# Hybrid S6/MoE/S5/MoE block: the expert layers moved by two slots, one sum and one normalisation moved to VectorE

## The chip, the cores and the metric

One NeuronCore of one Trainium2 chip runs the whole program. The metric is device time in microseconds, lower is better. Five engines take part: TensorE (PE; its weight loads are PEld), VectorE (DVE), ScalarE (ACT), GpSimd (POOL) and SyncE (SP), which issues nearly all DMAs.

## What is computed

The input x has 8 batches of 512 tokens with 128 channels, float32. Four residual layers follow each other, each on a layer-normed input:

```python
x = x + attn_a(layernorm(x))   # S6: silu(x Wi) -> d, B, C; delta = softplus(d Wdt)
                               # h_t = exp(delta_t A) h_{t-1} + delta_t B_t x_t, 256 channels x 64 states
                               # y = C * sum(h) + xs*Dp; y * silu(res) @ Wo; + residual; layernorm * gamma + beta
x = x + ffn(layernorm(x))      # 8 experts, the 2 largest logits, their softmax as weights
                               # sum_e weight_e * (silu(x W1_e) * (x W2_e)) @ W3_e
x = x + attn_b(layernorm(x))   # S5: 64 complex states, a diagonal scan, plus D*u
x = x + ffn(layernorm(x))      # the same experts again
```

All eight experts are computed for all tokens; `rt[:, 0]` holds each token's weight of each expert (zero for six of them).

## The kernel before, in words

**Turns and slots.** The S6 scan is the long part: 256 channels x 64 states x 512 steps are 128 scans ("pairs") of a 128x512 tile for each batch. The program runs 8 *turns*, one batch's 128 pairs each, and each pair is a *slot*. For pair k, ACT writes the decay `da = exp(dr * A)` into PSUM (L837), POOL the product `w = ur * br` of two pairs at once, a duo (L947), and DVE scans `h = da*h + w` (L1251). PE sums four scanned pairs into `ys` (`sum_states`, L633). The rings between them are short: `da` holds 4 pairs, `w` 5 duos, `h` 6 duos.

**What rides on the slots.** Every other piece of work is a generator that yields the slot at which it wants to be issued. `weave` (L210) puts them in each engine's own instruction stream: first the pair of the slot, then the tasks due, in the order gates, late, post, pre. Engines run their stream strictly in order and meet only through semaphores. A task whose slot is 128 or more is issued at the end of the turn, ahead of the next turn's first pair (the last loop of `weave`). In turn b the "pre" tasks prepare batch b+1 (layer norm, projections, delta, C), the "post" tasks do batch b-1 from `z` (the output projection) through the first MoE, S5 and the first part of the second MoE, and the "late" tasks finish the second MoE of batch b-2. After turn 7 two turns with no scan follow (the tail).

**The MoEs.** `MOE_AT` gives the slot where MoE 1 and MoE 2 begin (28 and 105). Each has four quarters of four tiles, 11 slots apart: `h` tiles (W1) and `g` tiles (W2) on PE (L565), silu on ACT (L785), the product `aq` on DVE (L1189). Expert e's output `y` is 8 pairs of matmuls on PE (L579); ACT scales it by the weights into `yk` (L798), POOL adds it to the residual tile (`expert_sums`, L890). `y`, `z` and the transposes share PSUM bank Y; the `h`/`g` tiles use banks H, G and sometimes Y. For MoE 2, tiles 8 to 15 and experts 3 to 7 are late: tiles 8 to 11 fall on slot 0 of the next turn, experts 3 to 7 on slots 0, 7, 14, 18, 23. Expert 2 of MoE 2 has slot 125 on PE and slot 131 in POOL's sum, so that sum stands at the end of the turn, before the next turn's first product.

**Last sum.** The 32nd sum of a turn (of pairs 124 to 127) is issued on PE by `tail()` (L641) at slot 128, thus ahead of the next turn's opening tiles. DVE's `take_sums(c, 1)` (L1127, slot 1 of the next turn) multiplies `ys` by the gate; PE's `z` (L583, slot 5) uses it; DVE adds the residual at slot 7 and takes the moments of layer norm 1 (L1093).

**Layer norms.** DVE takes moments, POOL computes rstd and -mean*rstd (`rstd`, L849), ACT applies them (`normalize`, L694) with four 128x128 activations. For layer norm 1 POOL then multiplies by gamma (L899) and adds the residual (L902).

**Routing.** DVE finds the two largest logits by a chain of 14 small operations (L1136). Intermediate tiles `R(1)`, `R(3)`, `R(5)` lie in SBUF, the others in the PSUM bank. The weights are built from a tanh of the half gap, as twice their value, and W3 is halved once: POOL does that in turn 0 (`scale_outputs`, L860, four operations of 128x512).

**Start.** Before turn 0 the projections of batch 0 run. DVE computes `delta` (L1120) behind the S5 matrix setup (L1029 to L1066, slot PRE_AT+10), and POOL's `du = delta * xs` (L878) waits until all four input tiles, the two of the residual branch (`sres`) included, are drained. SP stores delta and du to HBM (L357, L363) and loads them back spread over partitions (L368); the first product needs that load.

## Time and profile before

| | us |
|---|---|
| time, median of 3 runs (lowest, highest) | 1849.11 (1846.08, 1857.18) |
| profiled execution, its own time | 1861.63 |
| its span | 1859.7 |
| mean granted TensorE clock | 0.86 of full |
| first scan starts | 55.1 |
| turns 0 to 7, from first scan to last | 1641 |
| tail after the last scan | 164 |
| DVE, POOL, PE, ACT busy | 1514.5, 1513.9, 1351.0, 1281.5 |

The page has the engines' busy times, the span in 40 slices, the chain that ended last, and the costliest groups of instructions by line. The chain is spread thin: PE 27%, ACT 18%, DVE 15%, POOL 14%. "Idle" in a row is the time its engine stood still just before the instruction, with what released it. Consecutive DVE instructions overlap by about 0.08 us in the records, so a scan of 1.2 us advances the clock by 1.13.

### The profile page before, as it was taken

The numbers are of one execution on the slowest core, as the hardware profiler recorded it, in microseconds if no ns is written. First come the engines' busy times: TensorE is split into PE (matmuls) and PEld (weight loads), VectorE is DVE, ScalarE is ACT, GpSimd is POOL, SyncE is SP. The second block draws the span as 40 slices with busy tenths as digits, with TensorE's granted clock in tenths as the row PEclk, the third lists the DMA queues.
The fourth block names the chain that finished last, engine by engine and source line by source line (L and its number), as shares of the span: only waits on it lengthen the run. The fifth ranks groups of instructions, "written<-read, shape, count | busy, mean of one in ns | idle before, by whom it ended". The sixth has DMA issues, their size and how long they took to land.

```text
span 1859.7 us, 19053 instructions
## 1 busy us (share of the span) xinstructions
PE 1351.0 (73%) x5928; PEld 617.7 (33%) x5928; DVE 1514.5 (81%) x2105; ACT 1281.5 (69%) x2275; POOL 1513.9 (81%) x888
## 2 busy tenths in 40 slices
PE   4336458777886887778776878778787778668958
PEld 1001123234342343324342343324332343324535
DVE  4879988898889889898899888888888988895222
ACT  4547668687877778777777778777787777755423
POOL 0899999978998799977998899987998799983312
PEclk9557569889987989879897989879898898979979
DMA  3601411122111311132101401132111321100000
GB/s 87 212 34 71 164 46 51 49 91 97 57 40 48 148 51 33 54 104 96 55 25 50 162 29 51 49 106 81 51 51 49 102 85 52 46 29 1 7 1 6
DMA packets 38747, 121.89 MB, mean 66 GB/s; under 512 B 5875, under 2 KB 21110, under 8 KB 26358
## 3 DMA queue, kind: packets, MB, share of 16 engines
q1 hardware_dynamic: 37062, 120.67, 18.3%
q8 instruction: 47, 0.77, 0.2%
q14 instruction: 54, 0.44, 0.1%
q10 hardware_dynamic: 1584, 0.01, 0.0%
HBM read 109.13 MB, written 11.53 MB: 65 GB/s over the span
## 4 chain that ended last, share of the span: by engine, by line
PE 27%; ACT 18%; DVE 15%; POOL 14%; issue 8%; DVEq 0%; POOLq 0%; ACTq 0%
DVE h L1251 10%; POOL w L947 9%; PE bankH L565 8%; ACT da L837 5%; PE bankY L579 5%; PE bankG L565 5%; ACT yk L798 4%; ACT L837 3%; PE ys L633 2%; POOL x L890 2%; PE bankG L512 2%; DVE aq L1189 1%; PE bankY L559 1%; ACT L785 1%; ACT sq L785 1%
## 5 line engine op out<-in xcount | busy, mean ns | idle before, releaser
L1251 DVE TENSOR_TENSOR_SCAN h<-da,w 128x512 f32<-128x512 f32 x1024 | 1192.1, 1206 | 158.3 <-ACT da L837 133.0
L947 POOL TENSOR_TENSOR w<-ur,br 128x1024 f32<-128x1024 f32 x512 | 1193.6, 2365 | 33.1 <-DVE h L1251 21.2
L837 ACT ACTIVATE da<-dr,al 128x511 f32<-128x511 f32 x1024 | 681.9, 687 | 221.9 <-DVE h L1251 212.5
L633 PE MATMUL ys<-h,wsum 128*32 128x512 f32 x2048 | 320.9, 703 | 208.5 <-DVE h L1251 189.2
L565 PE MATMUL bankH<-nT,w 128*128 128x512 f32 x512 | 301.8, 673 | 89.7 <-DVE aq L1189 85.3
L890 POOL TENSOR_TENSOR x<-x,yk 128x512 f32<-128x512 f32 x128 | 163.1, 1274 | 211.2 <-ACT yk L798 210.6
L579 PEld LDWEIGHTS bankY<-w,aq 128*128 128x128 f32 x2048 | 262.8, 203 | 87.0 <-issue 65.0
L579 PE MATMUL bankY<-w,aq 128*128 128x128 f32 x2048 | 270.5, 289 | 12.4 <-DVE aq L1189 7.9
L565 PE MATMUL bankG<-nT,w 128*128 128x512 f32 x432 | 243.8, 648 | 24.6 <-DVE aq L1189 24.6
L798 ACT ACTIVATE yk<-bankY,rt 128x128 f32<-128x128 f32 x512 | 151.8, 364 | 121.5 <-PE bankY L579 107.8
L633 PEld LDWEIGHTS ys<-h,wsum 128*32 128x32 f32 x2048 | 42.9, 115 | 408.5 <-DVE h L1251 373.2
L565 PEld LDWEIGHTS bankH<-nT,w 128*128 128x128 f32 x512 | 87.0, 205 | 243.5 <-DVE aq L1189 147.9
L565 PEld LDWEIGHTS bankG<-nT,w 128*128 128x128 f32 x432 | 80.1, 203 | 163.9 <-issue 89.0
L512 PE MATMUL bankG<-xs,wx 128*128 128x512 f32 x64 | 44.3, 829 | 38.5 <-DVE sres L1115 37.7
L1189 DVE TENSOR_TENSOR aq<-tq,bankH 128x512 f32<-128x512 f32 x64 | 42.7, 667 | 35.3 <-PE bankH L565 35.3
L785 ACT ACT_TABLE_LOAD x55 | 70.6, 1283 | 1.0
L837 ACT ACT_TABLE_LOAD x54 | 69.3, 1283 | 1.0
L1189 DVE TENSOR_TENSOR aq<-tq,bankG 128x512 f32<-128x512 f32 x64 | 42.5, 665 | 32.2 <-PE bankG L565 32.1
L699 ACT ACTIVATE nrm<-x,nm,rs 128x128 f32<-128x128 f32 x96 | 39.4, 480 | 31.5 <-POOL nm L858 31.5
L852 POOL TENSOR_TENSOR var<-bag,eps 128x4 f32<-128x4 f32 x40 | 8.5, 212 | 59.0 <-DVE bag L1100 59.0
L785 ACT ACTIVATE tq<-bankH 128x512 f32<-128x512 f32 x64 | 38.3, 599 | 25.2 <-PE bankH L565 24.9
L785 ACT ACTIVATE sq<-bankH 128x512 f32<-128x512 f32 x64 | 38.2, 597 | 23.2 <-PE bankH L565 23.2
(187 smaller groups left out, 1135.8 us busy)
## 6 DMA issues: line engine op xcount, KB each, us to landing
br<-b_rows SPq DMA_DIRECT2D x64, 1024.0 KB, 5.0
dr<-d_rows SPq DMA_DIRECT2D x16, 1024.0 KB, 7.1
ur<-u_rows SPq DMA_DIRECT2D x16, 1024.0 KB, 8.4
d_rows<-vh SPq DMA_DIRECT2D x16, 256.0 KB
u_rows<-th SPq DMA_DIRECT2D x16, 256.0 KB
xnew<-in_L_attn_a_x_dram SPq DMA_DIRECT2D x8, 256.0 KB, 5.3
w<-in_L_ffn_W_dram SPq DMA_DIRECT2D x2, 1024.0 KB, 11.1
x<-in_L_attn_a_x_dram SPq DMA_DIRECT2D x8, 256.0 KB, 9.1
```

What stands on the lines that cost most here:

```text
L512: ins = nc.tensor.matmul(p[:, :], lhs(k), xs[:, k, :], start=(k == 0), stop=(k == 1))
L565: is_filled(t, f"{name}{m}_{n}", nc.tensor.matmul(p[:, :], wt[:, n // 2, n % 2 * 128:n % 2 * 128 + 128], nT[:, :], start=True, stop=True))
L579: ins = nc.tensor.matmul(p[:, a * 128:(a + 1) * 128], aq[:, (2 * n + k) % 4, a * 128:(a + 1) * 128], w3[:, n, k, :], start=(k == 0), stop= ...
L633: ins = nc.tensor.matmul(ys[32 * q:32 * q + 32, :], wsum[:, :], h[:, (DUOS * t.b + 2 * group + q // 2) % H_RING, q % 2, :], start=(n == 0) ...
L699: A(dst[:, a, :], src[:, a, :], ACT.Identity, bias=nm[:, k, a:a + 1], scale=rs[:, k, a:a + 1]).then_inc(normed[k], 1)
L785: A(zt[j % 4], p[:, :], ACT.Silu).then_inc(drained[BANK[f"h{m}_{j}"]], 1)
L798: ins = A(yk[:, a, :], p[:, a * 128:(a + 1) * 128], ACT.Copy, scale=rt[:, 0, a, e:e + 1])
L837: A(da[duo % D_RING][:, k % 2, 1:L], dr[:, half, q, 1:L], ACT.Exp, scale=nega[:, QUADS * half + q, n:n + 1]).then_inc(decay_ready, 1)
L890: G.tensor_tensor(total[:, :, :], total[:, :, :], yk[:, :, :], ALU.add).then_inc(added, 1)
L947: G.tensor_tensor(w[:, turn_duo % W_RING, :, :], ur[:, half, q:q + 2, :], br[:, chunk % B_RING, row:row + 1, :].to_broadcast([128, 2, L]), ...
L1189: drain(f"g{m}_{n}", V.tensor_tensor(aq[:, n % 4, :], zt[n % 4], p[:, :], ALU.mult))
L1251: V.tensor_tensor_scan(h[:, turn_duo % H_RING, k % 2, :], da[duo % D_RING][:, k % 2, :], w[:, turn_duo % W_RING, k % 2, :], 0.0, ALU.mult, ...
```

## The change

MoE 1 and 2 begin at slots 30 and 107, the pre tasks and layer norms 1 and 2 are two slots later too. Tiles 8 to 11 of the second MoE get slots 1, 1, 2, 2 (their `g` tiles 4, 5, 8, 9), late experts slots 5, 9, 16, 20, 25. The last sum of a turn moves on PE to slot 2 of the next turn. `take_sums` goes to slot 3, `z` to slot 6. A quarter's four silus are issued together. Layer norm 1 is applied by DVE with four `tensor_scalar`. The last expert of MoE 1 is weighted and added by DVE with four `scalar_tensor_tensor` on PSUM, so neither ACT nor POOL takes part. The weights have their own scale, W3 is not halved; for this the routing's `R(5)` (SBUF) is multiplied in SBUF by `rc`, which a new 128x4 `tensor_scalar` prepares. In the start, the S5 setup on DVE goes behind delta, and du of batch 0 waits for two input tiles only.

```diff
-MOE_AT = {1: 28, 2: 105}
+MOE_AT = {1: 30, 2: 107}
...
 FIRST_LATE_TILE, FIRST_LATE_OUTPUT = 8, 3
-LATE_OUTPUTS = {3: 0, 4: 7, 5: 14, 6: 18, 7: 23}
+LATE_OUTPUTS = {3: 5, 4: 9, 5: 16, 6: 20, 7: 25}
...
 THREE_STEPS = (2, 4, 7, 8)
+AT_TURN = ((1, 1, 2, 2), (4, 5, 8, 9))
+TAKE_AT = 3
...
-    at = silu_at(m, j) + step
-    return max(0, at - PAIRS) if is_late_tile(m, j) else at
+    at = silu_at(m, j)
+    if is_late_tile(m, j) and at < PAIRS + QUADS:
+        return AT_TURN[step > 0][j % 4]
+    return at - PAIRS + step if is_late_tile(m, j) else at + step
...
 GATES_AT, RES_AT = 44, 54
-PRE_AT = 70
+PRE_AT = 72
 SETUP_ROWS_AT = PRE_AT + 9
-SETUP_AT = PRE_AT + 10
-MATRICES_AT = PRE_AT + 11
+SETUP_AT = PRE_AT + 17
+MATRICES_AT = PRE_AT + 17
 TURN_AT = PRE_AT + 18
-SCALE_AT = 52
-LN_AT = [PRE_AT - 6, 7, 16, S5_AT, MOE_AT[2] - 8]
+LN_AT = [PRE_AT - 6, 9, 18, S5_AT, MOE_AT[2] - 8]
...
 GAP_STEP = 7
+SUMS = 2 * E - 1
+LAST_LAG = 2
...
 PE_STEPS = [
-    (5, "post", "Y", "z"), (MOE_AT[1] - 2, "post", "Y", "x1T"), (MOE_AT[1], "post", "Y", "lg1"),
+    (6, "post", "Y", "z"), (MOE_AT[1] - 2, "post", "Y", "x1T"), (MOE_AT[1], "post", "Y", "lg1"),
...
+def sums_before(c, m):
+
+    return SUMS * c + (E - 1) * (m - 1)
+
+def on_vector(m, e):
+
+    return m == 1 and e == E - 1
...
-    return sorted([(SLOT[f"h{m}_{j}"] + SILU_LAG, "h", j) for j in tiles_in(m, late)]
+    return sorted([(SLOT[f"h{m}_{j // 4 * 4}"] + SILU_LAG, "h", j) for j in tiles_in(m, late)]
                   + ([] if late else [(MOE_AT[m] + GAP_STEP, "gap", 0)])
-                  + [(weigh_slot(m, e, n), "y", 2 * e + n) for e in outputs_in(m, late) for n in range(2)],
+                  + [(weigh_slot(m, e, n), "y", 2 * e + n) for e in outputs_in(m, late) if not on_vector(m, e) for n in range(2)],
...
                 yield SLOT["y2_7"] + 8
-                sp.wait_ge(added, 2 * E * (c + 1))
+                sp.wait_ge(added, sums_before(c + 1, 1))
...
                             pe.wait_ge(drained[gated], t.before(f"g{m}_{2 * n + 1}") + 1)
-                        if n == 0:
-                            pe.wait_ge(outputs_scaled, QUADS)
...
             def scan(t):
-                def sum_states(group):
+                def sum_states(b, group):
                     n, half = group % PER_QUAD, group // PER_QUAD
-                    pe.wait_ge(scanned, PAIRS * t.b + 4 * group + 4)
+                    pe.wait_ge(scanned, PAIRS * b + 4 * group + 4)
                     if n == 0:
-                        if known(32 * t.b + group, 1):
+                        if known(32 * b + group, 1):
...
                         else:
-                            pe.wait_ge(ys_taken, 2 * t.b + half)
+                            pe.wait_ge(ys_taken, 2 * b + half)
                     for q in range(QUADS):
-                        ins = nc.tensor.matmul(ys[32 * q:32 * q + 32, :], wsum[:, :], h[:, (DUOS * t.b + 2 * group + q // 2) % H_RING, q % 2, :],
+                        ins = nc.tensor.matmul(ys[32 * q:32 * q + 32, :], wsum[:, :], h[:, (DUOS * b + 2 * group + q // 2) % H_RING, q % 2, :],
...
                 def pair(k):
-                    if k % 4 == SUM_AT % 4 and k >= SUM_AT:
-                        sum_states((k - SUM_AT) // 4)
-
-                def tail():
+                    if k % 4 != SUM_AT % 4:
+                        return
+                    if k >= SUM_AT:
+                        sum_states(t.b, (k - SUM_AT) // 4)
+                    elif not known(t.b, 1):
+                        sum_states(t.b - 1, PAIRS // 4 - 1)
+
+                def last_sum():
                     yield PAIRS
-                    for group in range((PAIRS - 1 - SUM_AT) // 4 + 1, PAIRS // 4):
-                        sum_states(group)
-
-                weave(pair, [tail()] + tasks_of(t, pre_a, post, late))
+                    sum_states(t.b, PAIRS // 4 - 1)
+
+                weave(pair, ([last_sum()] if t.b == NB - 1 else []) + tasks_of(t, pre_a, post, late))
...
                     copy_out(t, f"x{2 * m - 1}T", nT[:, :])
-                w0 = 3 * E * (2 * c + m - 1)
-                a0 = E * (2 * c + m - 1)
+                a0 = sums_before(c, m)
...
                 c = t.b - 1
-                yield from normalize(1, c, LN_AT[1], z, nrm)
...
-            def scale_outputs():
-
-                for n in range(QUADS):
-                    yield SCALE_AT + 3 * n
-                    if n == 0:
-                        pool.wait_ge(expert_loads, 16 * EXPERT_LOADS)
-                    part = w3[:, 2 * n:2 * n + 2, :, :].rearrange("p e k c -> p (e k c)")
-                    G.tensor_scalar(part, part, 0.5, None, ALU.mult).then_inc(outputs_scaled, 1)
...
                     if half == 0:
-                        for m in range(4):
+                        for m in range(2 if known(i, 1) else 4):
...
                 for e in outputs_in(m, is_late):
+                    if on_vector(m, e):
+                        continue
                     yield SLOT[f"y{m}_{e}"] + SUM_LAG
-                    pool.wait_ge(weighted, 3 * (E * (2 * c + m - 1) + e + 1))
+                    pool.wait_ge(weighted, 3 * (sums_before(c, m) + e + 1))
...
                     if e > 0:
-                        pool.wait_ge(added, E * (2 * c + m - 1) + e)
+                        pool.wait_ge(added, sums_before(c, m) + e)
...
-                weave(pair, [gates(t)] + ([scale_outputs()] if known(t.b, 1) else []) + tasks_of(t, pre_a, post, late))
+                weave(pair, [gates(t)] + tasks_of(t, pre_a, post, late))
...
                 V.tensor_tensor(rc[:, 3, :], largest[1], largest[0], ALU.subtract).then_inc(gap_ready, 1)
-                link(V.tensor_tensor(R(4), R(2), R(1), ALU.subtract))
-                link(V.tensor_tensor(R(5), R(2), R(1), ALU.add))
+                link(V.tensor_tensor(R(5), R(1), R(2), ALU.subtract))
...
                 v.wait_ge(gap_tanh_ready, 2 * c + m)
-                link(V.tensor_tensor(R(4), R(4), spread(rc[:, 2, :]), ALU.mult))
-                drain(f"lg{m}", V.tensor_tensor(rt[:, 0, :, :], R(4), R(5), ALU.add))
+                link(V.tensor_scalar(rc[:, 2, :], rc[:, 2, :], -0.5, 0.5, ALU.mult, ALU.add))
+                link(V.tensor_tensor(R(5), R(5), spread(rc[:, 2, :]), ALU.mult))
+                drain(f"lg{m}", V.tensor_tensor(rt[:, 0, :, :], R(5), R(2), ALU.add))
...
                 c = t.b - 1
-                yield from take_sums(c, 1, t, 1)
-                yield SLOT["z"] + 2
+                yield from take_sums(c, 1, t, TAKE_AT)
+                yield SLOT["z"] + 3
...
                 yield from moments(1, c, LN_AT[1], z)
+                yield LN_AT[1] + NORM_LAG
+                v.wait_ge(rstd_ready[1], 4 * c + 4)
+                for a in range(TT):
+                    V.tensor_scalar(nrm[:, a, :], z[:, a, :], rs[:, 1, a:a + 1], nm[:, 1, a:a + 1], ALU.mult, ALU.add).then_inc(normed[1], 1)
...
                 flat = lambda ap: ap[:, :, :].rearrange("p a c -> p (a c)")
+                last = f"y1_{E - 1}"
+                yield SLOT[last] + LAST_LAG
+                v.wait_ge(added, sums_before(c, 2))
+                p = got(t, last)
+                for a in range(TT):
+                    ins = V.scalar_tensor_tensor(x1[:, a, :], p[:, a * 128:(a + 1) * 128], rt[:, 0, a, E - 1:E], x1[:, a, :], ALU.mult, ALU.add)
+                    if a < TT - 1:
+                        ins.then_inc(last_added, 1)
+                drain(last, ins)
                 yield LN_AT[3]
-                v.wait_ge(added, E * (2 * c + 1))
+                v.wait_ge(last_added, (TT - 1) * (c + 1))
+                v.wait_ge(drained[BANK[last]], t.before(last) + 1)
```

## Rows read from the trace of the kernel before

**Rows 1.** Stretches of turn 0 and turn 3: length, then busy us by engine, PEclk, DMA.
```profile
55.05:222.10 167.05, 70.47 (x276) 11.07 (x276) 151.28 (x144) 102.07 (x153) 165.92 (x80) 0.57 0.30 106
...
639.67:851.40 211.73, 164.57 (x741) 76.88 (x742) 186.46 (x250) 161.42 (x287) 188.50 (x111) 0.90 0.20 70
```

**Rows 2.** Groups by line: busy us, mean ns, idle before and releaser.
```profile
L947 POOL TENSOR_TENSOR w<-ur,br 128x1024 f32<-128x1024 f32 x512 | 1193.6, 2365 | 33.1 <-DVE h L1251 21.2 <-issue 11.9
L1251 DVE TENSOR_TENSOR_SCAN h<-da,w 128x512 f32<-128x512 f32 x1024 | 1192.1, 1206 | 158.3 <-ACT da L837 133.0 <-issue 16.1 <-POOL w L947 6.3
...
L867 POOL TENSOR_SCALAR w<-w 128x512 f32<-128x512 f32 x4 | 6.1, 1528 | 0.0
```

**Rows 3.** Timeline, from turn 2 into turn 3: start, us, engine, line.
```profile
631.07 0.66 DVE L1189 TENSOR_TENSOR aq<-tq,bankH 128x512 f32<-128x512 f32 x1
...
632.74 1.95 PE L579 MATMUL bankY<-w,aq 128*128 128x128 f32 x16
...
634.73 1.14 ACT L798 ACTIVATE yk<-bankY,rt 128x128 f32<-128x128 f32 x4 [1.14 <-PE bankY L579]
...
636.00 1.26 POOL L890 TENSOR_TENSOR x<-x,yk 128x512 f32<-128x512 f32 x1 [1.73 <-ACT yk L798]
...
639.67 1.22 DVE L1251 TENSOR_TENSOR_SCAN h<-da,w 128x512 f32<-128x512 f32 x1 [1.16 <-ACT da L837]
```

**Rows 4.** Timeline, first 24 slots of turn 3.
```profile
638.57 1.06 PE L633 MATMUL ys<-h,wsum 128*32 128x512 f32 x8 [2.88 <-DVE h L1251]
...
656.98 1.14 ACT L798 ACTIVATE yk<-bankY,rt 128x128 f32<-128x128 f32 x4 [3.25 <-PE bankY L579]
...
662.93 1.64 ACT L699 ACTIVATE nrm<-z,nm,rs 128x128 f32<-128x128 f32 x4
...
666.60 1.22 DVE L1251 TENSOR_TENSOR_SCAN h<-da,w 128x512 f32<-128x512 f32 x1 [3.82 <-ACT da L837]
...
679.72 2.35 POOL L947 TENSOR_TENSOR w<-ur,br 128x1024 f32<-128x1024 f32 x1
```

**Rows 5.** Timeline of the start, up to the first product.
```profile
33.16 0.69 DVE L1120 TENSOR_TENSOR vh<-th,bankG 128x512 f32<-128x512 f32 x1 [0.22 <-DVE nrm L1064]
...
38.18 2.49 POOL L878 TENSOR_TENSOR th<-vh,xs 128x512 f32<-128x512 f32 x2 [28.19 <-ACT sres L715]
...
46.38 0.55 SPq L368 DMA_DIRECT2D ur<-u_rows  x1
...
48.31 0.41 DVE L1089 COPY mc<-bankY 128x256 f32<-128x256 f32 x1
...
52.60 13.86 POOL L947 TENSOR_TENSOR w<-ur,br 128x1024 f32<-128x1024 f32 x6 [11.94 <-issue]
```

**Rows 6.** DVE operations with all operands in SBUF: timeline, then groups by form.
```profile
38.17 1.30 DVE L1080 SCALAR_TENSOR_TENSOR cosT<-cosT,s5w,rT 128x8 f32<-128x8 f32 x1
...
L1075 DVE TENSOR_SCALAR rT<-sinT,s5w 128x256 f32<-128x256 f32 x1 | 0.4, 353 | 0.0
L1080 DVE SCALAR_TENSOR_TENSOR cosT<-cosT,s5w,rT 128x128 f32<-128x128 f32 x1 | 0.4, 351 | 0.0
...
L1075 DVE TENSOR_SCALAR rT<-sinT,s5w 128x128 f32<-128x128 f32 x1 | 0.3, 286 | 0.0
```

**Rows 7.** Timeline around the end of the routing, MoE 1 and MoE 2.
```profile
689.08 16.27 POOL L947 TENSOR_TENSOR w<-ur,br 128x1024 f32<-128x1024 f32 x7
...
700.19 0.19 DVE L1174 TENSOR_TENSOR bankY<-bankY,rc 128x32 f32<-128x32 f32 x1
...
812.68 13.92 POOL L947 TENSOR_TENSOR w<-ur,br 128x1024 f32<-128x1024 f32 x6
...
825.61 0.19 DVE L1174 TENSOR_TENSOR bankY<-bankY,rc 128x32 f32<-128x32 f32 x1
```

**Rows 8.** Timeline of turn 3 at slot 77: moments of layer norm 3.
```profile
769.66 0.87 DVE L1097 BATCH_NORM_STATS2 bst<-x 128x6 f32<-128x128 f32 x4 [1.88 <-POOL x L890]
```

**Rows 9.** The chain that ended last, in the tail.
```profile
1777.52 1.27 POOL x L890
```

More of the change, by code:

```diff
@@ L278, in hybrid_kernel @@
         ones_ready = sem("ones_ready"); angles_ready = sem("angles_ready"); rates_ready = sem("rates_ready"); matrices_ready = sem("matrices_ready")
-        setup_done = sem("setup_done"); outputs_scaled = sem("outputs_scaled"); setup_chain = sem("setup_chain"); rows_spread = sem("rows_spread")
+        setup_done = sem("setup_done"); setup_chain = sem("setup_chain"); rows_spread = sem("rows_spread")
         matrices_turned = sem("matrices_turned"); setup_a = sem("setup_a"); diagonal_a = sem("diagonal_a")
@@ L298, in hybrid_kernel @@
         gap_ready = sem("gap_ready"); gap_tanh_ready = sem("gap_tanh_ready"); routed = sem("routed")
-        weighted = sem("weighted"); added = sem("added")
+        weighted = sem("weighted"); added = sem("added"); last_added = sem("last_added")
         sin_ready = sem("sin_ready"); turned_ready = sem("turned_ready"); diagonal_scanned = sem("diagonal_scanned"); real_ready = sem("real_ready")
```

## The prediction

> **What bounds the kernel now.** I read the page's busy times first, then the stretches of single turns, the lead of `da` and `w` over each scan in the timeline, and last the chain of waits. In a middle turn of 211.73 us DVE is busy 186.46 and POOL 188.50: neither alone is the bound, both lose some 25 us per turn to waits on each other, ACT and PE. In turn 0, which has no MoE, POOL is busy 165.92 of 167.05 us, so there every microsecond of POOL counts [rows 1]. Per pair DVE needs 1.13 us (a scan of 1.206 less the overlap), per duo POOL 2.365 [rows 2]. So with anything else to do POOL is late, and after a turn's opening it runs without a gap for some 20 slots: the product of slot 24 starts at 679.72 and ends 0.09 us before its scan [rows 4]. The turn's start hangs on one chain. The last-but-two `aq` of the second MoE ends at 631.73; PE makes expert 2's output from 632.74, ACT weighs it at 634.73, POOL adds it at 636.00, and only then, in POOL's own order, comes the first product (2.36), so the first scan starts at 639.67, 7.94 us after that `aq` [rows 3]. The chain the change aims at is beside it: PE waits 2.88 us for the last scan before the turn's last sum, and the opening tiles stand behind that sum; later scan 14 waits 3.82 us because ACT waited 3.25 for expert 4 and then had four silus and the norm (1.64) ahead of the decay [rows 4].
>
> **The change part by part.** The sum is made against the profiled execution, 1861.6 us (span 1859.7 and 1.9 around it), which lies 12.5 us above the median of the runs; the difference is carried over to the median, 1849.1.
>
> *Start.* Delta (L1120) starts at 33.16 behind the S5 matrix setup and du at 38.18, released by `sres`, 28.19 us of idle before it. The logarithm that delta needs is done about 3.1 us before 33.16. So du of half 0 can end near 32.1 instead of 39.4. The store of du takes 6.9 us to the issue of its load (39.47 to 46.38), the load 6.2 to the first product at 52.60 [rows 5]. That gives a first product near 45.3; some of it is lost because the loads of delta and du now run at once. DVE is the other end: its setup ends at 48.72 [rows 5], and it will end about 1.2 later since DVE idles for the logarithm, so scan 0 starts at 49.9 at the earliest, 5.2 us sooner than 55.1. Between 5.2 and 7.3, I take 6.0, as POOL is the bound of turn 0 and its head start counts. -6.0.
>
> *W3 unscaled.* Four POOL operations of 1.528 go from turn 0 [rows 2], which POOL bounds [rows 1]; nothing hides them. -6.1.
>
> *The boundary of the turns (turns 2 to 7, six times).* With MoE 2 two slots later, expert 2's output has slot 127 and its sum still stands ahead of the next product. The chain of rows 3 is unchanged, 7.94 us from the `aq` to scan 0; but this `aq` now has slot 124, so beside the chain DVE has 3 scans and 2 `aq` (4.6 us) where it had 5 scans and 2 `aq` (6.8). Its idle before scan 0 grows from 1.16 to about 3.4: +2.25. What the moved last sum frees is not on this chain: the opening tiles no longer wait for scan 127, but their silus come behind decay 4 instead of decay 3, which needs scan 0, and scan 0 waits for POOL. Expert 3 moves from slot 0 to 5, its weighing to 8 and 9, and `z` waits for that in bank Y, then expert 4 waits for `z`. Going through the orders with the durations of rows 3 and 4 I get expert 4's weighing some 3.5 us late for POOL, where POOL waited 1.5, of which 0.8 stays. The norm taken from ACT (1.64 of the 3.82) does not help past slot 24, where POOL's product ends last [rows 4]. The norm's four `tensor_scalar` cost DVE 0.2 us each net (0.286 a piece) [rows 6] and may have to wait for products, another 0.5. Together +3.5. The other end is what the change is meant to give, the 2.88 us that PE waited [rows 4]: -2.9 per turn. The links of rows 3 all stand in program order, so the upper end is nearer, but POOL waits again later in the turn (at the outputs of both MoEs), which may take some of it up. I take half the upper end: 6 x 1.7 = +10.2. In turn 1, which has no late tasks, only the norm counts: two products can lie in its way, I take +1.5.
>
> *The routing's new operations (turns 1 to 7, both MoEs).* Before, each operation of this chain had one operand in the PSUM bank; now `R(5) * rc` reads two tensors in SBUF, and the 128x4 `tensor_scalar` ahead of it reads and writes SBUF. The trace shows what such an operation does beside POOL: L1080 with 128x8 elements takes 1.30 us when du (38.18, two of 1.25) runs, and 0.351 with 128x128 when POOL is idle [rows 5, 6]. It ended with POOL's operation. In a turn POOL's operations are the 2.36 us products. In MoE 1 seven of them run end to end from 689.08, one each 2.32 us; the routing's last two operations begin at 700.19. There the first of the new pair would wait to 700.7, the second, issued after it, to 703.0: +2.7. In MoE 2 the last of six products ends at 826.6, and these operations begin at 825.61: the first waits 1.0, the second finds POOL waiting for scans: +1.2 [rows 7]. Behind the waiting operation on DVE stand the scans, and for these wait ACT (four decays ahead), PE's sums and the weights of expert 0; POOL can run ahead only five duos. So nothing hides it. Low end 0 (the operations fall into gaps), upper end two products at each place, 9.4 per turn; for the `tensor_scalar` alone between 0 and one product. I take 3.9, from the very positions of rows 7: 7 x 3.9 = +27.3.
>
> The Trainium skill, "SBUF — State Buffer", section "Who interferes with whom", says that a VectorE instruction with two SBUF inputs contends with a GpSimd one that reads SBUF, that a `tensor_scalar` between SBUF tensors can enter a form that contends too, and that the loser blocks for the whole instruction. For two inputs the trace agrees (1.30 against 0.35 us, rows 6). No row shows it for `tensor_scalar`; the rule would give the forecast, rows of two-input operations alone the fourth case below. Before this change no DVE operation of a middle turn, as far as I see, was of either kind.
>
> *Last expert of MoE 1 on DVE (turns 1 to 7).* DVE waits 1.88 us at slot 77 for POOL's sum [rows 8]. That goes; four `scalar_tensor_tensor` come in, 0.27 to 0.35 each by the nearest row [rows 6], say 1.2. They have one SBUF tensor, so POOL is not in the way, and PE's output is there when DVE reaches them. ACT (1.1) and POOL (1.26) are freed where neither ends last. 7 x -0.7 = -4.9. In the tail nothing else runs: ACT's 1.14 and POOL's 1.27 [rows 3, 9] for 1.2: -1.3. The grouped silus keep the number of table loads, and only change order by a slot: 0, hidden behind the wait for the tiles.
>
> Sum: -6.0 - 6.1 + 10.2 + 1.5 + 27.3 - 4.9 - 1.3 = +20.7. That is 1882 on the profiled execution's scale and **1870** on the runs'.
>
> **The rivals.** *First, the boundary at its full price:* the walk's +3.5 is not taken up again. +10.8 more, 1881. For it: POOL has no gap up to slot 30. Against: its later waits. This is slower, decided once expert 2's sum still ends after about 636 in its turn's frame. *Second, no stalls:* the new DVE operations find their way between products. Then the 27.3, the 1.5 and six times 0.5 go: -11, 1838. For it: a single pair of rows of 1.3 us carries the stall, from the start and with other shapes. *Third, the opening gains as well:* PE's wait was the true start of the chain, and a turn becomes 2.9 us shorter rather than 1.2 longer: 1838 less 6 x 4.1, 1813. For it: the chain of waits does run through the last sum in every turn; against it, rows 3. *Fourth, only two-input operations stall:* `tensor_scalar` is free, so in MoE 1 the product of `R(5)` waits to 700.7 and not 703.0, +0.5, in MoE 2 +1.2, and the norm costs no wait: 7 x 1.7 instead of 27.3, less 4.5: about 1850. *The change not doing what it says* is part of the forecast: the last sum is behind the opening tiles, and they still start late.
>
> **How the numbers follow.** Forecast 0.45, first rival 0.13, second 0.22, third 0.12, fourth 0.08. One per cent, about what a measurement of this kernel can tell from no change, is 18.5 us: 1830.6 and 1867.6. The forecast's own range is 1856 to 1888, of which 0.29 lies above 1867.6 and 0.16 below. Slower by over 1%: 0.29 + 0.13 = 0.42. Within: 0.16 + 0.22 + 0.08 = 0.46. Faster: the third, 0.12. The range 1826 to 1886 leaves out the third case and the top of the first.
>
> **What would show it.** Right: the first scan at 49 to 50 us; turn 0 some 6 us shorter; DVE operations of the routing (128x4, 128x32) of 1 to 2.5 us instead of 0.2, some of the norm's above 1; idle of 3 us before scan 0 of turns 2 to 7; middle turns of about 217 us; no wait on POOL before the moments of layer norm 3. Wrong: all those operations at 0.2 to 0.3 us (second or third case), or middle turns under 210 us, which would say that the last sum was the start of the chain.

## The result, and the profile of the changed kernel

The changed kernel takes **1903.82 us** (median of 4 runs, 1902.75 to 1905.19), the kernel before, run beside it, 1853.14 us (4 runs, 1846.08 to 1857.36): ratio 1.0273, 95% interval 1.0249 to 1.0298. That is slower by 50.7 us, where 1870 with a range up to 1886 was predicted. The profiled execution has a span of 1903.4 us.

The stretches of turn 0 and turn 3, as in [rows 1] (length, busy us of PE, PEld, DVE, ACT, POOL, then PEclk, DMA share, GB/s):

```profile
58.94:213.00 154.06, 70.49 (x276) 11.36 (x276) 149.40 (x143) 101.97 (x153) 151.08 (x73) 0.58 0.26 90
643.75:865.45 221.70, 172.35 (x740) 78.01 (x740) 194.44 (x257) 158.60 (x278) 187.18 (x110) 0.88 0.20 66
```

Turn 0 begins 3.9 us later than in [rows 1] and is 13.0 us shorter; turn 3 is 10.0 us longer, with 8.0 us more of busy DVE, and PE is busy 7.8 us longer for the same instructions (x740 for x741), at a granted clock of 0.88 for 0.90. So two things are to be found: what DVE does longer, and why PE is slower.

The groups by form that the change touched on DVE (busy us, mean ns):

```profile
L1211 DVE TENSOR_SCALAR nrm<-z,rs,nm 128x128 f32<-128x128 f32 x32 | 31.2, 1032 | 4.7 <-POOL nm L872 4.7
L1180 DVE TENSOR_SCALAR rc<-rc 128x4 f32<-128x4 f32 x16 | 23.8, 1491 | 0.0
...
L1181 DVE TENSOR_TENSOR rt<-rt,rc 128x32 f32<-128x32 f32 x16 | 9.4, 585 | 0.6
L1222 DVE SCALAR_TENSOR_TENSOR x<-bankY,rt,x 128x128 f32<-128x128 f32 x32 | 8.8, 338 | 4.5 <-PE bankY L592 4.5
```

Unhindered, L1180 takes 0.16 us and L1181 0.19 (so they stand in the tail, where no product runs). 16 x 0.35 is 5.6 us; they were busy 33.2. The routing's stalls are thus **27.6 us**, and the prediction had 27.3. L1222, the last expert on DVE, has one tensor in PSUM and never stalls.

DVE in turn 3 around MoE 1's routing, and below it POOL:

```profile
711.53 2.80 DVE L1180 TENSOR_SCALAR rc<-rc 128x4 f32<-128x4 f32 x1
714.37 0.19 DVE L1181 TENSOR_TENSOR rt<-rt,rc 128x32 f32<-128x32 f32 x1
```

```profile
702.72 11.59 POOL L954 TENSOR_TENSOR w<-ur,br 128x1024 f32<-128x1024 f32 x5
721.31 1.27 POOL L897 TENSOR_TENSOR x<-x,yk 128x512 f32<-128x512 f32 x1 [7.00 <-ACT yk L813]
```

The 128x4 operation of four numbers a partition ends at 714.33, 0.02 us behind the last of these five products (714.31; with two ahead of those shown, the row is of seven, from 698.10). It began in the fourth of the five, and though that one ended at 712.00 it did not enter there. What hangs on the weights is late with it: POOL waits 7.00 us for expert 0's weighing, for 1.79 at the same place in the kernel before. PE in the same turn:

```profile
694.28 0.91 PE L479 MATMUL bankY<-ident,nrm 128*128 128x128 f32 x4 [3.68 <-ACT yk L813]
695.12 1.93 PE L646 MATMUL ys<-h,wsum 128*32 128x512 f32 x8
696.98 1.88 PE L574 MATMUL bankY<-wg,nT 128*128 128x8 f32 x8
698.71 2.06 PE L580 MATMUL bankH<-nT,w 128*128 128x512 f32 x2
700.56 1.91 PE L580 MATMUL bankG<-nT,w 128*128 128x512 f32 x2
...
705.21 1.02 PE L580 MATMUL bankH<-nT,w 128*128 128x512 f32 x2
```

The same pair of matmuls takes 1.02 us at full clock (2.4 GHz, granted clock 1.00 from 704.9 on) and 1.91 at the lower level (1.2 GHz, 0.50 from 695.2 to 703.9). PE had waited 3.68 us, and then worked at half speed for nine microseconds. Before the change the wait at this place was 2.49 and the slow stretch some five:

```profile
685.29 1.08 PE L464 MATMUL bankY<-ident,nrm 128*128 128x128 f32 x4 [2.49 <-ACT yk L798]
687.07 1.87 PE L559 MATMUL bankY<-wg,nT 128*128 128x8 f32 x8 [0.69 <-ACT nT L661]
688.79 2.05 PE L565 MATMUL bankH<-nT,w 128*128 128x512 f32 x2
690.64 1.59 PE L565 MATMUL bankG<-nT,w 128*128 128x512 f32 x2
692.06 1.02 PE L565 MATMUL bankH<-nT,w 128*128 128x512 f32 x2
```

The norm on DVE stalls as well: in each of turns 2 to 7 two of the four L1211 take 1.69 and 2.40 us instead of 0.33. The moments of layer norm 3 no longer wait for POOL [rows 8]. The idle time before scan 0 of turn 3 is 3.41 us, for 1.16 in [rows 3] and 3.4 in the prediction:

```profile
643.75 2.34 DVE L1272 TENSOR_TENSOR_SCAN h<-da,w 128x512 f32<-128x512 f32 x2 [3.41 <-issue]
```

Last the start. POOL, then DVE:

```profile
29.74 2.49 POOL L883 TENSOR_TENSOR th<-vh,xs 128x512 f32<-128x512 f32 x2 [19.50 <-DVE vh L1127]
44.38 11.68 POOL L954 TENSOR_TENSOR w<-ur,br 128x1024 f32<-128x1024 f32 x5 [12.15 <-issue]
```

```profile
44.45 2.42 DVE L1087 SCALAR_TENSOR_TENSOR cosT<-cosT,s5w,rT 128x128 f32<-128x128 f32 x1
46.80 2.42 DVE L1088 SCALAR_TENSOR_TENSOR sinT<-sinT,s5w,tq 128x128 f32<-128x128 f32 x1
49.14 2.29 DVE L1089 SCALAR_TENSOR_TENSOR s5w<-s5w 128x1 f32<-128x1 f32 x1
51.47 2.40 DVE L1082 TENSOR_SCALAR rT<-sinT,s5w 128x256 f32<-128x256 f32 x1
53.78 2.42 DVE L1083 TENSOR_SCALAR tq<-cosT,s5w 128x256 f32<-128x256 f32 x1
...
58.94 3.45 DVE L1272 TENSOR_TENSOR_SCAN h<-da,w 128x512 f32<-128x512 f32 x3 [0.36 <-DVE mc L1096]
```

The first product stands at 44.38 (45.3 was predicted; [rows 5] has 52.60), but five small operations of DVE's chain each wait for one of the five products: 11.95 us for what takes 1.6 unhindered. Scan 0 starts at 58.94, not at 49.9.

### The profile page after: what moved, and what is told of

Read it like the earlier page. It is cut to its first block, busy times and chain, and to the rows that moved or that the text cites. A ratio compares the mean times of both kernels' runs of the same rounds, so it can differ in the third digit from the quotient of the medians.

```text
span 1903.4 us, 19040 instructions
## 1 busy us (share of the span) xinstructions
PE 1388.1 (73%) x5928; PEld 622.8 (33%) x5928; DVE 1584.3 (83%) x2169; ACT 1259.1 (66%) x2211; POOL 1498.0 (79%) x876
## 4 chain that ended last, share of the span: by engine, by line
PE 30%; DVE 18%; ACT 16%; POOL 14%; issue 9%; DVEq 0%; POOLq 0%; ACTq 0%
POOL w L954 11%; DVE h L1272 11%; PE bankH L580 9%; PE bankG L580 6%; ACT da L851 5%; PE bankY L592 4%; DVE aq L1196 3%; ACT L851 3%; ACT yk L813 3%; PE ys L646 2%; POOL x L897 2%; PE bankG L527 2%; PE bankY L580 1%; PE bankY L574 1%; ACT sq L800 1%
## 5 line engine op out<-in xcount | busy, mean ns | idle before, releaser
L646 PE MATMUL ys<-h,wsum 128*32 128x512 f32 x2048 | 327.1, 716 | 173.6 <-DVE h L1272 144.2
L580 PE MATMUL bankH<-nT,w 128*128 128x512 f32 x512 | 315.0, 701 | 120.1 <-DVE aq L1196 91.6
L897 POOL TENSOR_TENSOR x<-x,yk 128x512 f32<-128x512 f32 x120 | 152.7, 1272 | 257.5 <-ACT yk L813 257.3
L592 PEld LDWEIGHTS bankY<-w,aq 128*128 128x128 f32 x2048 | 254.9, 198 | 105.8 <-issue 58.5
L592 PE MATMUL bankY<-w,aq 128*128 128x128 f32 x2048 | 261.4, 282 | 25.9 <-DVE rt L1182 12.9
L580 PE MATMUL bankG<-nT,w 128*128 128x512 f32 x432 | 262.6, 693 | 17.8 <-DVE aq L1196 17.6
L813 ACT ACTIVATE yk<-bankY,rt 128x128 f32<-128x128 f32 x480 | 141.7, 362 | 126.8 <-PE bankY L592 121.4
L580 PEld LDWEIGHTS bankH<-nT,w 128*128 128x128 f32 x512 | 92.8, 212 | 265.4 <-DVE aq L1196 154.3
L479 PE MATMUL bankY<-ident,nrm 128*128 128x128 f32 x96 | 24.6, 406 | 73.5 <-ACT nrm L715 48.9
L527 PE MATMUL bankG<-xs,wx 128*128 128x512 f32 x64 | 49.9, 922 | 28.7 <-DVE sres L1122 27.0
```

Source lines behind the costliest of these rows:

```text
L527: ins = nc.tensor.matmul(p[:, :], lhs(k), xs[:, k, :], start=(k == 0), stop=(k == 1))
L580: is_filled(t, f"{name}{m}_{n}", nc.tensor.matmul(p[:, :], wt[:, n // 2, n % 2 * 128:n % 2 * 128 + 128], nT[:, :], start=True, stop=True))
L592: ins = nc.tensor.matmul(p[:, a * 128:(a + 1) * 128], aq[:, (2 * n + k) % 4, a * 128:(a + 1) * 128], w3[:, n, k, :], start=(k == 0), stop= ...
L646: ins = nc.tensor.matmul(ys[32 * q:32 * q + 32, :], wsum[:, :], h[:, (DUOS * b + 2 * group + q // 2) % H_RING, q % 2, :], start=(n == 0), ...
L813: ins = A(yk[:, a, :], p[:, a * 128:(a + 1) * 128], ACT.Copy, scale=rt[:, 0, a, e:e + 1])
L897: G.tensor_tensor(total[:, :, :], total[:, :, :], yk[:, :, :], ALU.add).then_inc(added, 1)
```

## The experiments

Ratios are of the runs to those of the kernel before beside them, in brackets the 95% interval; the medians of the kernel before lay at 1848 to 1855 us, its single runs between 1846 and 1858, so gains of 4 to 6 us stand at the edge of what can be told. The code is cut to the lines that matter; semaphores, counts and names that go with them are left out.

### The routing

**b1**: on the kernel before, the routing of the change and W3 unscaled.

```diff
-link(V.tensor_tensor(R(4), R(2), R(1), ALU.subtract))
-link(V.tensor_tensor(R(5), R(2), R(1), ALU.add))
+link(V.tensor_tensor(R(5), R(1), R(2), ALU.subtract))
...
+link(V.tensor_scalar(rc[:, 2, :], rc[:, 2, :], -0.5, 0.5, ALU.mult, ALU.add))
-link(V.tensor_tensor(R(4), R(4), spread(rc[:, 2, :]), ALU.mult))
-drain(f"lg{m}", V.tensor_tensor(rt[:, 0, :, :], R(4), R(5), ALU.add))
+link(V.tensor_tensor(R(5), R(5), spread(rc[:, 2, :]), ALU.mult))
+drain(f"lg{m}", V.tensor_tensor(rt[:, 0, :, :], R(5), R(2), ALU.add))
```

> The kernel before with the new routing (R(5) in SBUF, the tensor_scalar on rc) and W3 unscaled, nothing else. My theory: the three SBUF-only operations of the routing wait behind GpSimd's products, and what follows (rt, the weights, the first experts) is late with them: about 4 us of stall in a turn as predicted and as much again for what waits behind, so 7 x 4 to 7 us less 6 us at the start, about 1853 + 34 = 1887 us (1875 to 1900). Rival (the schedule around the turn's boundary and the two-slot shift cost the time, the routing's stalls are hidden in idle time): the start's gain alone stays, about 1847 us.

Measured: 1892.0 us, 1.0209 [1.0180, 1.0239].

**b6**: as b1, but only the `tensor_scalar` has nothing in PSUM (shown against the kernel before).

```diff
-link(V.tensor_tensor(R(5), R(2), R(1), ALU.add))
...
+link(V.tensor_scalar(rc[:, 2, :], rc[:, 2, :], 0.5, 0.5, ALU.mult, ALU.add))
 link(V.tensor_tensor(R(4), R(4), spread(rc[:, 2, :]), ALU.mult))
-drain(f"lg{m}", V.tensor_tensor(rt[:, 0, :, :], R(4), R(5), ALU.add))
+drain(f"lg{m}", V.tensor_tensor(rt[:, 0, :, :], R(4), R(1), ALU.add))
```

> The kernel before with W3 unscaled and a routing whose two-input operations all have an operand in PSUM, the 128x4 tensor_scalar on rc the only operation left with nothing in PSUM. Theory A (one waiting operation is enough; the tensor_scalar alone misses whole gaps, as its 2.80 and 4.40 us in the changed kernel): most of the routing kernel's excess stays, 1875 us (1868 to 1887). Theory B (the two-input operations in SBUF are what costs, each some 2 us): 1852 us within 5.

Measured: 1887.6 us, 1.0192 [1.0145, 1.0239].

**b5**: as b1, but the halving stands on ScalarE, so the product of `R(5)` is the only operation with nothing in PSUM (the write of `R(5)` ahead of it reads `R(2)` there and takes 0.17 us). Shown against b1.

```diff
-link(V.tensor_scalar(rc[:, 2, :], rc[:, 2, :], -0.5, 0.5, ALU.mult, ALU.add))
+A(rc[:, 2, :], rc[:, 2, :], ACT.Copy, scale=-0.5, bias=0.5).then_inc(gap_tanh_ready, 1)
```

> The kernel before with W3 unscaled and R(5) in SBUF: two of the routing's two-input operations have nothing in PSUM, and the halving of the tanh stands on ScalarE, so the tensor_scalar is gone. Theory A (what costs is mostly the operation that comes first after the tanh and meets a product, of whatever kind): one stall of about 2.3 us in a turn at MoE 1, 1865 us (1856 to 1880). My prediction's rival 4 priced exactly this operation at 2.1 us a turn: -6 + 15, 1862 us. Theory B (only the tensor_scalar misses gaps and is dear): 1850 us or less.

Measured: 1879.9 us, 1.0156 [1.0101, 1.0211].

**b7**: as b6, with the halving on ScalarE (shown against b6).

```diff
-link(V.tensor_scalar(rc[:, 2, :], rc[:, 2, :], 0.5, 0.5, ALU.mult, ALU.add))
+A(rc[:, 2, :], rc[:, 2, :], ACT.Copy, scale=0.5, bias=0.5).then_inc(gap_tanh_ready, 1)
```

> As b6, but the halving of the tanh stands on ScalarE as a second small operation, so no operation of the routing on VectorE is without an operand in PSUM. Both theories of the port: the excess is gone and W3 unscaled stays, 1848 us (1844 to 1852). Rival (it is the routing's longer chain, on whatever engine, that makes the weights late): 1865 us or more.

Measured: 1842.9 us, 0.9968 [0.9937, 0.9998].

b1 against b7 is the routing's price on the old schedule: 0.0241, or 45 us. b6, which differs from b7 by the place of one operation of 128x4 alone, pays 0.0224 (41 us), b5 0.0188 (35 us). So one operation of the kind pays most of it. (b6 came out 0.6 us above its range, b7 1.1 below.) Both of my theories on which kind is dear were too narrow: either kind waits, and a single one can wait as long as two. And these operations were two in b1 and one in b5, not three and two as expected there. The DVE of b6 in turn 5 and of b5 in turn 3, and POOL beside each:

```profile
1139.10 5.25 DVE L1171 TENSOR_SCALAR rc<-rc 128x4 f32<-128x4 f32 x1
```

```profile
1128.08 16.24 POOL L945 TENSOR_TENSOR w<-ur,br 128x1024 f32<-128x1024 f32 x7
```

```profile
705.66 5.24 DVE L1173 TENSOR_TENSOR rt<-rt,rc 128x32 f32<-128x32 f32 x1
```

```profile
694.64 16.21 POOL L947 TENSOR_TENSOR w<-ur,br 128x1024 f32<-128x1024 f32 x7
```

The first ends at 1144.35 beside a row of seven products that ends at 1144.32, the second at 710.90 beside one that ends at 710.85: both passed two ends of products (each 2.36 us) and entered at the third. That third end is the end of POOL's row: behind it POOL stands still for some 7 us, since next in its order is expert 0's sum, which needs the weights that this very chain makes. The traces have 13 routing operations that passed an end (4 in the changed kernel, 2 in b1, 4 in b6, 3 in b5), and all 13 entered only when POOL's row was through. The others entered at the first end; the shortest waits, in other turns of b5 and b6, took 0.43 to 0.62 us. Where it did so in b1, the product of `R(5)` right behind it waited for the next one (2.29 us).

The stalls in b1's trace (20.8 us for L1171 and 13.5 for L1172, less 5.6) are 28.7 us; the price is 45. The rest, 16 us, is what comes on top (12 in b6, whose stalls are 29.0 us, 14 in b5, 21.0). It does not follow the length of the stalls: b1's turn 3, with 6.2 us of them, takes 218.7 us, its turn 4, with 3.4, takes 218.2. In b1's turn 4 DVE waits longer for the second opening tile than before (2.84 us for 1.21), and PE there reads

```profile
852.75 1.93 PE L631 MATMUL ys<-h,wsum 128*32 128x512 f32 x8 [2.88 <-DVE h L1249]
854.61 1.88 PE L565 MATMUL bankH<-nT,w 128*128 128x512 f32 x2
```

where the kernel before has, at the same place,

```profile
850.29 1.06 PE L633 MATMUL ys<-h,wsum 128*32 128x512 f32 x8 [2.88 <-DVE h L1251]
851.29 1.12 PE L565 MATMUL bankH<-nT,w 128*128 128x512 f32 x2
```

The same work after the same wait, at half the clock: 1.6 us on the chain that opens the turn. That the late weights bring the lower clock is not shown: b8, which has none of these stalls, has slow opening tiles too. What the 12 to 16 us consist of stays open.

### The norm

**b2**: on the kernel before, only the norm on DVE (four `tensor_scalar` `nrm<-z` at `LN_AT[1] + NORM_LAG`, as in the change).

> The kernel before with the normalisation of the attention norm on VectorE instead of ScalarE, nothing else. My theory: two of its four small operations stall (1.69 and 2.40 us instead of 0.33 where the changed kernel was read), some 3.4 us of VectorE's time in each of 7 turns, half of it given back because ScalarE and the tiles behind it start earlier: about +12 us, 1865 us (1858 to 1877). Rival (the stall falls into idle time): 1853 us within 4.

Measured: 1865.3 us, 1.0079 [1.0051, 1.0106].

**a1**: the changed kernel with a routing without stalls (15 operations, each two-input one with an operand in PSUM). **a2**: a1 with the norm back on ScalarE.

```diff
-link(V.tensor_tensor(R(5), R(1), R(2), ALU.subtract))
-link(V.tensor_scalar(rc[:, 2, :], rc[:, 2, :], -0.5, 0.5, ALU.mult, ALU.add))
...
+link(V.tensor_tensor(R(4), R(2), R(1), ALU.subtract))
+link(V.scalar_tensor_tensor(R(5), R(2), 0.5, R(1), ALU.mult, ALU.add))
...
+link(V.tensor_tensor(R(4), R(4), spread(rc[:, 2, :]), ALU.mult))
+link(V.tensor_tensor(R(4), R(4), R(1), ALU.subtract))
+drain(f"lg{m}", V.scalar_tensor_tensor(rt[:, 0, :, :], R(4), 0.5, R(5), ALU.mult, ALU.add))
```

> The changed kernel with the PSUM-side routing of a2 and everything else as changed, the attention norm on VectorE too. Against a2 (1865) it tells the norm's price inside the changed schedule: theory, as alone in b2 (+11 us), 1876 us (1871 to 1881). Rival (the moved slots give the norm idle time to stand in): 1865 us within 3. Against the changed kernel (1904) it tells the routing's: 28 us by the theory, 39 us by the rival.

> The changed kernel with a routing of 15 operations whose two-input operations all have an operand in PSUM (no tensor_scalar on rc) and with the attention norm back on ScalarE; schedule, last expert on VectorE, W3 unscaled and start stay changed. My theory: nearly all of the excess goes, 1904 less some 45 = about 1858 us (1848 to 1866). Rival (schedule): 1890 us or more.

Measured: a1 1866.5 us, 1.0064 [1.0043, 1.0084]; a2 1864.6 us, 1.0071 [1.0045, 1.0097]. The norm's stalls cost 15 us by the ratio (11 by the medians) on the old schedule, where b2's trace has 4.0 us of them in a turn, and nothing that can be measured on the new one, where a1's has 3.4; the rival was right there. The changed kernel less a1 is 0.0209, 39 us: the routing.

### The start

**b3**: on the kernel before, the start alone. **b9**: b3 with POOL's first product held until DVE's chain is through.

```diff
-SETUP_AT = PRE_AT + 10
-MATRICES_AT = PRE_AT + 11
+SETUP_AT = PRE_AT + 17
+MATRICES_AT = PRE_AT + 17
...
-for m in range(4):
+for m in range(2 if known(i, 1) else 4):
```

```diff
 pool.wait_ge(setup_done, 1)
+pool.wait_ge(chain_done, 1)
```

> The kernel before with the start's new order alone (delta ahead of the S5 setup, du waiting for two inputs instead of four). My theory now: GpSimd's first products lie beside VectorE's chain of small SBUF-only operations and stretch it, so scan 0 comes no earlier, or up to 5 us later, and what the head start of the products gives back in turn 0 (some 7 us) just pays for it: 1851 us (1848 to 1856). Rival (my prediction's own term, the products' head start alone): scan 0 four to five us earlier, 1847 us.

> As b3 (the start's new order alone), but GpSimd's first product waits until VectorE's chain of small operations is through, so the products have no head start and nothing lies beside the chain. Theory (the products stretch the chain by some 8 us in b3): the chain ends near 46 us instead of 58, scan 0 starts near 50 us, turn 0 is 167 us long again instead of 160.7, the time 1852 us. Rival (the chain is late by itself, since delta now stands ahead of it): scan 0 at 58 us or later and turn 0 at 167 us, 1860 us.

Measured: b3 1855.8 us, 1.0004 [0.9982, 1.0026], scan 0 at 58.9, turn 0 160.7 us. b9 1852.6 us, 0.9993 [0.9979, 1.0007], scan 0 at 50.8, turn 0 165.7 us, and its first product at 48.40:

```profile
48.40 6.94 POOL L948 TENSOR_TENSOR w<-ur,br 128x1024 f32<-128x1024 f32 x3 [16.30 <-DVEq L1093]
```

Without products beside it the chain ends at 48.11 instead of 58.57, with delta at 28.8 in both: the products were the cause. The whole start of the kernel before moves by itself: delta, at 33.16 in [rows 5], stands at 29.14 in b4's trace, whose start is the same code, the first product at 49.07 and scan 0 at 51.5 instead of 55.1. Part of what I meant to gain was such a late start. And b9 gains nothing beside it either: with the setup behind delta its chain ends 3.4 us later than b4's (44.68), where 1.2 was reckoned.

### The last expert on DVE

**b4**: on the kernel before, that part alone. **b8**: b7 and b4 together.

```diff
...
+for a in range(TT):
+    ins = V.scalar_tensor_tensor(x1[:, a, :], p[:, a * 128:(a + 1) * 128], rt[:, 0, a, E - 1:E], x1[:, a, :], ALU.mult, ALU.add)
```

> The kernel before with the last expert of MoE 1 added on VectorE from PSUM, nothing else. The prediction: -0.7 us in each of 7 turns, 1848 us. Rival (the wait it takes away was not the one that sets the turn's pace, since the turns of s1 without it and of a2 with it are equally long, 215.1 and 215.0 us): 1853 us within 3.

> The kernel before with W3 unscaled by the halving on ScalarE and the last expert of MoE 1 added on VectorE: the two edits that gained alone (0.9968 and 0.9980). If they add up, 1853 less 6 less 4 = 1843 us. Rival (both fill the same idle time): 1847 us or more.

Measured: b4 1849.5 us, 0.9980 [0.9962, 0.9997]; b8 1843.5 us, 0.9964 [0.9948, 0.9980]. Whether the two gains add up is not told: their product, 0.9948, is the very end of b8's interval, and b8's own ratio is no better than b7's (0.9968). In the profile the kernel before has turns of 211.7 and of 214.8 us (two of the latter among turns 2 to 6), b4 and b8 only such of 211.6.

### The schedule

**s1**: the changed kernel with all but the schedule (the silus issued together included) as before. **s2**: s1 with the last sum at its own turn's end. **s3**: the kernel before with the last sum alone moved. **s4**: s1 with the two-slot shift undone. **s6**: s1 with the opening tiles by the rule of before and each silu behind its own tile again.

```diff
 s2, undone in s1:
-elif not known(t.b, 1):
-    sum_states(t.b - 1, PAIRS // 4 - 1)
 s4:
-MOE_AT = {1: 30, 2: 107}
-LATE_OUTPUTS = {3: 5, 4: 9, 5: 16, 6: 20, 7: 25}
-PRE_AT = 72
+MOE_AT = {1: 28, 2: 105}
+LATE_OUTPUTS = {3: 0, 4: 7, 5: 14, 6: 18, 7: 23}
+PRE_AT = 70
 s6:
-return AT_TURN[step > 0][j % 4]
+return max(0, at - PAIRS)
```

> The changed kernel with routing, W3's scaling, the attention norm on ScalarE, the last expert's sum on ScalarE and GpSimd and the start's order all as before, so that only the turn's last sum, the new slots of the opening tiles and the shift by two slots are left. My theory: the boundary's idle time of 3.4 us stays about what it was, and the schedule costs 1 to 2 us in a turn: about 1853 + 10 = 1863 us (1853 to 1870). Rival (the schedule is what costs the time): 1890 us or more, with the routing kernel near the time of before.

> As s1, with the turn's last sum back at the end of its own turn, so that of the schedule only the new slots of the opening tiles and the shift by two slots are left. Theory 1 (the two-slot shift of the MoEs and of the late tiles costs what s1 lost, the sum's place nothing): 1870 us within 4. Theory 2 (the sum behind the next turn's opening tiles is what costs): 1853 us. Theory 3 (the moved sum gains, and the shift costs more than s1 shows): 1875 us or more.

> The kernel before with the turn's last sum alone moved behind the next turn's opening tiles (its result taken from the bank at slot 3 instead of 1), the slots of before kept. Theory 1: 1853 us within 4. Theory 2: 1865 us or more. Theory 3: 1845 us or less.

> As s1 (1870), but the two-slot shift is undone: MoEs, late outputs, norms and the projections ahead stand at the slots of before, and the turn's last sum, z and the opening tiles at their new ones. Theory S (the shift costs it): 1854 us within 4. Theory O (the opening tiles' new slots and the silus' earlier ones cost it, whatever slots follow): 1868 us within 4.

> As s1 (1870, its turns 215.0 us), but the opening tiles' slots are worked out by the rule of before, under the two-slot shift: all four first tiles at slot 1 and their gated halves at 3, 4, 8 and 9 instead of 1, 1, 2, 2 and 4, 5, 8, 9. Theory O (the rearranged opening tiles cost the 3.4 us of a turn): 212 us a turn, 1854 us. Theory S (pushing everything behind the opening back by two slots costs it, the tiles' places inside do not matter): 215 us a turn, 1870 us.

Measured: s1 1870.0 us, 1.0093 [1.0061, 1.0125]; s2 1869.7, 1.0104 [1.0060, 1.0147]; s3 1850.4, 1.0009 [0.9989, 1.0029]; s4 1883.8, 1.0158 [1.0136, 1.0181]; s6 1869.4, 1.0103 [1.0078, 1.0128]. The moved sum is free, on the old slots (s3) and on the new (s1 and s2 are alike).

Against s3 each of the two other moves costs by itself. The shift costs 17 us (s6 against s3, ratios 1.0103 and 1.0009; `z` stands a slot later too). The new tile slots without the shift, together with the grouped silus and the later `z`, cost 28 us (s4 against s3, 1.0158 and 1.0009); a4 and a5 below differ by the same three and are 26 us apart. Both moves together cost no more than the shift alone (s1). So theory O was right for the old slots and theory S for the new ones, and s4 lies above either's range. Which of its three parts is the dear one was not separated. In s4 expert 3's output stands ahead of the tiles; the first 16 slots of turn 3 take 34.31 us there for 29.60 in s3:

```profile
637.32:671.63 34.31, 27.50 (x126) 14.73 (x124) 23.69 (x31) 23.47 (x41) 27.38 (x18) 0.90 0.24 91
629.41:659.01 29.60, 25.80 (x138) 14.31 (x138) 23.74 (x32) 22.95 (x41) 25.95 (x17) 1.00 0.25 101
```

Its turns 3 to 6 are 215.0 us, like those of s1; what it loses more lies in turn 7 (5 us) and in the tail (10 us), and why stays open.

The turn's opening on PE in s1, and in s3:

```profile
637.47 1.13 PE L581 MATMUL bankH<-nT,w 128*128 128x512 f32 x2 [1.63 <-DVE aq L1209]
...
639.38 1.07 PE L649 MATMUL ys<-h,wsum 128*32 128x512 f32 x8
644.74 2.07 PE L581 MATMUL bankH<-nT,w 128*128 128x512 f32 x2 [4.29 <-ACT tq L803]
646.60 1.92 PE L581 MATMUL bankG<-nT,w 128*128 128x512 f32 x2
```

```profile
630.94 1.13 PE L565 MATMUL bankH<-nT,w 128*128 128x512 f32 x2 [1.78 <-ACT tq L788]
...
632.76 1.95 PE L579 MATMUL bankY<-w,aq 128*128 128x128 f32 x16
```

The shift takes expert 3's output from the head of the turn, and PE waits 4.29 us for the first silu (scan 0 is late, hence decay 4, hence the silu). Behind that wait the clock is at its lower level (0.50 granted from 644.8 to 648.2) and the next two tiles take nearly twice their time. This is read from the rows; no run changes the wait alone. The stretch of the first 16 slots of turn 3 and the one of slots 32 to 48, in s1 and then in the kernel before:

```profile
640.82:671.69 30.87, 25.35 (x126) 14.40 (x127) 23.05 (x30) 21.69 (x38) 25.45 (x16) 0.89 0.11 35
696.75:722.67 25.92, 21.82 (x90) 8.49 (x88) 23.36 (x33) 21.70 (x38) 25.11 (x13) 0.93 0.25 82
```

```profile
639.67:669.46 29.79, 26.31 (x134) 14.72 (x134) 23.58 (x32) 23.07 (x41) 26.00 (x17) 1.00 0.27 101
696.76:720.20 23.44, 19.31 (x96) 8.83 (x96) 21.94 (x24) 19.57 (x35) 21.25 (x12) 1.00 0.17 57
```

Both are longer, 1.1 and 2.5 us, and both have lost the full clock. In the changed kernel they show 0.89 and 0.83.

### Put together

**a4**: the changed kernel with b7's routing, the norm on ScalarE, start and slots as before; moved sum, tile slots, grouped silus, `z` at slot 6, last expert and W3 unscaled stay. **a5**: b8 with the moved sum (s3's edit), which is a4 with the tiles, silus and `z` as before.

> The changed kernel with its four dear parts mended: the halving of the tanh on ScalarE, the attention norm on ScalarE, the start's order and all slots but the opening's as before; last sum moved, last expert on VectorE and W3 unscaled stay. If the shift was what a2 still paid for (theory S), this lies at b8's time, 1843 us; if the opening tiles are (theory O), 1858 us.

> b8 (W3 unscaled with the halving on ScalarE, last expert on VectorE) with the turn's last sum moved as well, all slots of before: the parts of the change that did not cost by themselves, together. Since the sum was free alone (s3): 1843 us within 3. If the schedule's loss comes from the sum meeting the other parts: 1850 us or more.

Measured: a4 1859.3 us, 1.0040 [1.0012, 1.0068], nearest to the theory that the opening tiles cost, and 26 us above a5, which differs by the tiles, their silus and `z` alone. a5 **1832.6 us, 0.9900 [0.9869, 0.9932]**, 1.0% faster than the kernel before, and faster than either expectation. The sum that was free alone gains 11 us beside the other two parts (b8 1843.5, its interval and a5's apart). The turn's opening and turn 3 in a5:

```profile
630.40 1.12 PE L577 MATMUL bankH<-nT,w 128*128 128x512 f32 x2 [1.78 <-ACT tq L797]
...
634.96 1.07 PE L643 MATMUL ys<-h,wsum 128*32 128x512 f32 x8
```

```profile
628.86:838.05 209.19, 162.02 (x740) 76.11 (x740) 187.13 (x251) 160.72 (x285) 187.19 (x110) 0.92 0.20 71
```

In b8 the first two tile rows of the opening stand behind the sum, at 1.85 and 1.91 us, and DVE waits 2.81 us for the second tile's pair; in a5 the first two take 1.12 and 1.02 and it waits 1.56. The first 16 slots of turn 3 take 31.4 us at a granted clock of 0.95 in b8 and 29.6 at 1.00 in a5; six such turns are 11 us. Over the whole turn both have 0.92. This too is read from the rows.

## Why the prediction was wrong

The likeliest case was right in its direction and in most of its mechanisms, but not in its sizes: the start failed in its mechanism, and what the boundary, the norm and the routing cost was mis-sized. All but the norm err to the same side, and the routing's price alone is 12 us over its term.

- **Start (-6.0): failed.** The first product came at 44.38, as early as worked out, but from a start of the kernel before that is by itself up to 4 us earlier than the one read (49.07 in b4 for 52.60), so it gained 4.7 us and not 7.3. The step that failed is "it will end about 1.2 later since DVE idles for the logarithm": DVE's chain, all in SBUF, would lie beside those very products. I had the stall in [rows 6], in the same chain, and applied it to the routing alone. b3: +0.7 us; b9 shows the products as the cause, and that the chain is 3.4 us later even without them.
- **W3 unscaled (-6.1): right.** Turn 0 is 161.5 us in b7 against 167.0, and b7 gains 6 us, with an interval from nearly 0 to 12.
- **Boundary and opening (+10.2): right in sign, too small.** 3.41 us of idle before scan 0 is as predicted, and so is the walk's +3.5 (turns of 215.0 us in s1 for 211.6). The step that failed is "I take half the upper end": nothing took it up again, and s1 and s2 cost 17 and 19 us, near the full 6 x 3.5 = 21. Part of the delay is matmuls at half the clock behind a longer wait, which the walk, made with the durations of [rows 3, 4], did not have.
- **Norm: stalls mis-sized, effect right.** "Another 0.5" a turn is 3.4, but it costs 11 to 15 us only on the old schedule (b2) and nothing on the new one (a1, a2).
- **Routing (+27.3): the stalls right in their sum, 27.6 in the trace; their price wrong, 39 us** (45 on the old schedule). Two steps failed. "The first would wait to 700.7, the second to 703.0" took the next end of a product as the place of entry, one for each operation; the runs show that, or one operation alone that stays out until POOL's row is through. In the changed kernel MoE 1's stalls are 2.3 to 4.2 us a turn, 21.7 in all for 18.9 predicted, and MoE 2's 5.8 for 8.4: that the sums meet within 0.3 us is luck. And "so nothing hides it" stopped at the stall itself: 11 us come on top of it here, 12 to 16 in b1, b5 and b6, and what they consist of is open. The fourth rival, that only two-input operations stall, fell with b6.
- **Last expert (-4.9): right in sign.** b4 gains 4 us, with an interval from 1 to 7, and b8 shows no more than b7. (In the term for the tail, 1.14 and 1.27 less 1.2 is 1.2 and not 1.3.)

The terms as measured: start +1, W3 -6, schedule +17, norm 0, routing +39, last expert -4, together +47 for +50.7. The routing and the schedule, 56 us, are shown by runs that change them alone; where parts meet (b8, a5, s1) they do not simply add, so the sum is a guide and no proof.

The Trainium skill ("SBUF — State Buffer", section "Who interferes with whom") says that of a VectorE and a GpSimd instruction that contend whoever issues first gets the shared pair of ports "for the whole instruction" and the other fully blocks. The trace agrees in kind, for `tensor_scalar` too (b6), but its stalls of 5.1 us span more than the 2.36 us of one product.

## What to carry to other kernels

A small VectorE operation with all tensors in SBUF, beside a row of back-to-back GpSimd ones, should be costed at up to the rest of their row, not at one; keep an operand in PSUM (a1: 39 us less), or put it on ScalarE (b7 against b6: the same arithmetic, 41 us less). That holds for setup code as well as soon as another edit starts GpSimd earlier. A wait added on TensorE is dearer than its length where the matmuls behind it then run at the lower clock (s1), so a move is priced by the granted clock of its stretch as well. And parts of a schedule do not add: a move that is free alone may gain beside others (a5), and one that costs 28 us alone may cost nothing beside another (s4, s1), so each is tried in company before it is kept or dropped.
